# Local attention: probabilities times values on four 64x64 tiles, issued right behind the scores

## Chip, cores, metric

The kernel runs on 1 core of one Trainium2 chip. The time is device microseconds of one execution; lower is better. Engines are named as in the profile: PE is TensorE's matmul side, PEld its weight loads, DVE is VectorE, ACT ScalarE, POOL GpSimd, SP SyncE (it only issues DMAs here).

## The reference, cut to the part that is changed

The whole program is four layers on x of [8, 256, 128]: additive attention, a stack of six local-attention layers with feed-forward, a state-space layer and a mixture of experts. The change is in the stack. Per layer:

```python
qkv = x @ Wqkv                       # 16 heads of 64
q, k = l2norm(q) * qs, l2norm(k) * ksc
q = q * cos * scale + rotate_half(q) * sin * scale
k = k * cos * inv + rotate_half(k) * sin * inv
# windows of 32 positions; each sees itself and the window before it
sim = einsum('bhwie,bhwje->bhwij', bq, bk2) * 8.0
attn = softmax(where(mask, -max, sim), -1)
out = einsum('bhwij,bhwje->bhwie', attn, bv2)   # "mix" below
x = out.reshape(b, n, 1024) @ Wo + x            # then shift, layer norm, feed-forward with gelu
```

## The kernel before

Everything is float32, and the stream lies in SBUF transposed, channels on the 128 partitions. `local_attention` (L295) works in **units** of 512 tokens, which are two batches of 256. Four units a layer and six layers make 24 units, numbered i = 0 to 23. A unit is cut into eight **slots** j = 0 to 7, one per pair of heads. The program of every engine is written out by hand, slot by slot (`slot` at L529 for PE, L643 for ACT, L715 for POOL, L793 for DVE), each engine runs its list strictly in that order, and semaphores (`need`) tie the engines together. A hardware loop runs two units per turn; the first and the last unit stand outside it. A slot is a software pipeline in which four pairs of heads are in work at once:

- `scores(j)` (L439): two bf16 matmuls put the mask into PSUM banks 4 and 5 (L450), then 32 small float32 matmuls (L457), 64 rows by 32 columns of the array, add queries times keys. They wait for the rotated and normalised keys (`qk`) and for the probabilities of j-1, which leave the same banks.
- `project(j+2)` (L423): the two projection matmuls of 512 columns, q into bank 0 (L430) and k into bank 1 (L431). In slots 6 and 7 they belong to the next unit.
- `values(j+2)` (L406): the values of 128 tokens for half of the heads, four matmuls of 256 columns (L418), bank 2. Eight of them make the value tile `f_v` of a unit.
- `mix(j-2)` (L469): probabilities times values, 16 matmuls with 64 rows and 64 columns (L478), into bank 7.
- `turn(j-1)` (L462): four transposes of the probabilities (L466), bank 6.
- `norms(j+2)` (L433): the sums of squares of q and k, two matmuls of 512 columns (L436, L437), in banks 0 and 1 again. They need the squares that ACT makes of the copied projection.

Some slots carry work of the unit before (k = i-1) as well: slots 0 and 1 three matmuls each of the output projection (L491), slot 2 its last two and, on DVE, the residual and the token shift; slot 3 the mean of the layer norm (L498), slot 4 its variance (L504), slot 5 the first gate and hidden matmul (L511, L518), slot 6 two gates and a hidden, slot 7 a hidden and the second feed-forward matmul (L525). In slots 0 to 5 the order on PE is scores, project, values, mix, turn, norms. In slot 6 the mix stands ahead of the projection, in slot 7 the values do.

ACT does in a slot: `raw_copy` (L607, copies both projections out of PSUM, and L610 squares them), the exponential of the scores (L663) in place in banks 4 and 5, `value_copy` (L599), `out_copy` of the mix's result (L635), `spread` (L625, L626, L628: puts the transposed probabilities of the eight pairs of windows, 96 columns each, into `f_ptz`), and `inverse_norm` (L616 logarithm, L618 exponential). In slot 4 it then takes the logarithm and exponential of the variance (L678, L680).

DVE does in a slot: `soft_a` (L765 maximum, L769 subtraction), `normalise` (L757) of the next pair, `soft_b` (L776 sum, L779 reciprocal, L781 product, the probabilities), `rotate` (L747, L750); at the end of slot 2 L816 and the shift (L726, L728); at the end of slot 4 it scales the feed-forward input (L828), which waits for ACT's L680. POOL does the other half of the rotation (L709, L713).

## Time and profile before

| | |
|---|---|
| three runs | 2627.81, 2629.06, 2631.60 us; median 2629.06 |
| profiled execution, first to last instruction | 2628.3 us, inside the range of the runs; no other time is given for it |
| PE busy | 2396.4 us, 91% of the span |
| DVE / ACT / POOL busy | 1953.7 / 1795.4 / 1082.1 us |
| mean granted TensorE clock | 0.971 of full |

"Busy" is the union of an engine's instructions. A matmul's duration in a row is from its first read to a modelled end, so that consecutive rows overlap; the distance of two starts tells what the engine was held for. Each float32 matmul of the program is two PE instructions. In the timeline a row is a start and a duration in us, the engine, the line, the operation, the tiles, and in brackets the idle time just before it with what ended it. In the rows on windows each engine has its busy time and number of instructions, and PEclk is the granted clock as a share of 2.4 GHz.

### The profile page before, as it was taken

The page shows a single profiled execution, that of the slowest core. Times are in us where ns is not written, and L with a number is a line of the kernel's source. Part 1 is how long each engine was busy: PE and PEld are TensorE (multiplying, and loading weights), DVE is VectorE, ACT ScalarE, POOL GpSimd, SP SyncE. Part 2 cuts the span into 40 slices and gives each one's busy share as a digit, 9 for nine tenths or more (in the row PEclk, how much of TensorE's full clock was granted, in tenths as well). Part 3 has the DMA queues.
Part 4 walks back from the last instruction along what each step waited for, and adds up shares of the span by engine and source line. Part 5 has one row for each costly group of instructions (what it writes and reads, how often), then busy time and mean ns, then how long its engine had stood idle before and what let it go on. Part 6 is the DMA issues. An engine that isn't in the chain of part 4 may idle for free. (4 is left out here: it accounts for less than half of the span.)

```text
span 2628.3 us, 62460 instructions
## 1 busy us (share of the span) xinstructions
PE 2396.4 (91%) x24940; PEld 1259.7 (48%) x24940; DVE 1953.7 (74%) x2595; ACT 1795.4 (68%) x2593; POOL 1082.1 (41%) x461
## 2 busy tenths in 40 slices
PE   7799999999999999999999999999999877767778
PEld 2355555555554555555545455555555422222355
DVE  5678777788677777787778777788777658999542
ACT  4677767777677776777767777677677666545533
POOL 0354444444444444444444444444444204556130
PEclk8899999999999999999999999999999989999989
DMA  0100000000000000000000000000000010000001
GB/s 21 54 2 2 2 26 10 10 2 2 15 22 11 2 2 14 22 11 2 2 14 14 19 2 2 14 14 15 5 2 2 2 37 0 0 0 0 18 23 41
DMA packets 16047, 29.92 MB, mean 11 GB/s; under 512 B 3616, under 2 KB 6064, under 8 KB 15664
## 3 DMA queue, kind: packets, MB, share of 16 engines
q1 hardware_dynamic: 15760, 25.78, 3.1%
q8 instruction: 218, 3.57, 0.5%
q14 instruction: 69, 0.57, 0.1%
HBM read 24.73 MB, written 1.05 MB: 10 GB/s over the span
## 5 line engine op out<-in xcount | busy, mean ns | idle before, releaser
L709 POOL TENSOR_TENSOR f_rot<-f_raw,f_tabc 128x1024 f32<-128x1024 f32 x192 | 452.6, 2357 | 694.7 <-DVE f_qk L757 302.4
L713 POOL TENSOR_TENSOR f_rot<-f_rot,f_shuf 128x1024 f32<-128x1024 f32 x192 | 453.1, 2360 | 470.0 <-DVE f_shuf L750 470.0
L607 ACT ACTIVATE f_raw<-f_ps 128x1024 f32<-128x1024 f32 x192 | 196.5, 1023 | 324.9 <-PE f_ps L431 324.9
L478 PEld LDWEIGHTS f_ps<-f_ptz,f_v 64*64 64x64 f32 x6144 | 260.2, 133 | 93.7 <-issue 93.7
L478 PE MATMUL f_ps<-f_ptz,f_v 64*64 64x96 f32 (+1 forms) x6144 | 286.7, 243 | 1.5 <-ACT f_ptz L628 1.4
L776 DVE TENSOR_REDUCE f_sum<-f_ps 128x8 f32<-128x512 f32 x192 | 131.8, 686 | 185.6 <-ACT f_ps L663 185.5
L747 DVE STREAM_SHUFFLE f_shuf<-f_raw 128x1024 f32<-128x1024 f32 x192 | 255.2, 1329 | 0.0
L757 DVE SCALAR_TENSOR_TENSOR f_qk<-f_rn,f_rot 128x1024 f32<-128x1024 f32 x192 | 233.5, 1216 | 28.8 <-POOL f_rot L713 28.8
L430 PE MATMUL f_ps<-f_xs,f_wq 128*128 128x512 f32 x384 | 220.7, 657 | 24.3 <-DVE f_xs L728 21.0
L750 DVE TENSOR_TENSOR f_shuf<-f_shuf,f_tabs 128x1024 f32<-128x1024 f32 x192 | 236.7, 1233 | 7.6
L616 ACT ACTIVATE f_rn<-f_ps 128x1024 f32<-128x1024 f32 x192 | 198.8, 1035 | 39.5 <-PE f_ps L437 39.0
L618 ACT ACTIVATE f_rn<-f_rn,k_lift 128x1024 f32<-128x1024 f32 x192 | 220.6, 1149 | 6.3
L457 PE MATMUL f_ps<-f_qk 64*32 64x64 f32 x12288 | 195.1, 220 | 18.0 <-issue 18.0
L1136 POOL TENSOR_TENSOR s_prod<-s_state,s_cs 128x1024 f32<-128x1024 f32 x64 | 151.7, 2371 | 145.2 <-DVE s_state L1214 145.2
L418 PE MATMUL f_ps<-f_wv,f_xs 128*64 128x256 f32 x1536 | 210.5, 395 | 0.0
L765 DVE TENSOR_REDUCE f_max<-f_ps 128x8 f32<-128x512 f32 x192 | 131.8, 686 | 105.1 <-PE f_ps L457 103.7
L610 ACT ACTIVATE f_sq<-f_raw 128x1024 f32<-128x1024 f32 x192 | 203.1, 1058 | 6.1
L436 PE MATMUL f_ps<-f_sq,f_same 128*128 128x512 f32 x384 | 197.7, 597 | 6.2 <-ACT f_sq L610 6.2
L431 PE MATMUL f_ps<-f_xs,f_wk 128*128 128x512 f32 x384 | 203.1, 611 | 0.0
L437 PE MATMUL f_ps<-f_sq,f_same 128*128 128x512 f32 x384 | 197.0, 595 | 0.0
L457 PEld LDWEIGHTS f_ps<-f_qk 64*32 64x32 f32 x12288 | 161.9, 106 | 60.2 <-issue 60.2
L491 PE MATMUL f_ps<-f_o,f_wo 128*128 128x512 f32 x384 | 183.8, 612 | 0.0
(267 smaller groups left out, 3961.4 us busy)
## 6 DMA issues: line engine op xcount, KB each, us to landing
e_w<-in_e_w SPq DMA_DIRECT2D x16, 256.0 KB, 2.8
f_wq<-in_f_wq SPq DMA_DIRECT2D x12, 256.0 KB, 2.8
f_wk<-in_f_wk SPq DMA_DIRECT2D x12, 256.0 KB, 3.2
f_wv<-in_f_wv SPq DMA_DIRECT2D x12, 256.0 KB, 3.4
f_wo<-in_f_wo SPq DMA_DIRECT2D x6, 512.0 KB, 3.1
f_w<-in_f_w SPq DMA_DIRECT2D x6, 341.0 KB, 3.1
s_dx<-in_k_pick SPq DMA_DIRECT2D x1, 1536.0 KB, 9.3
f_w<-in_f_w SPq DMA_DIRECT2D x6, 192.0 KB, 3.8
```

The costliest lines, as they stand in the source:

```text
L418: mm = pe.matmul(view(ps, 2 * CH + 256 * r, [1, 256], p0=64 * h, rows=64), xs[:, at:at + 64], view(wv, CH * (q // 4) + 64 * h, [128, 4], [ ...
L430: pe.matmul(bank(0), wq[:, 128 * j:128 * j + 128], xs[:, :], start=True, stop=True)
L431: pe.matmul(bank(1), wk[:, 128 * j:128 * j + 128], xs[:, :], start=True, stop=True).then_inc(sem["a_mm"], 1)
L457: mm = pe.matmul(view(ps, (4 + h) * CH + (w // 4) * 64, [1, 64], p0=WIN * (w % 4), rows=WIN), t[64 * h:64 * h + 64, WIN * w:WIN * w + WIN] ...
L478: mm = pe.matmul(view(ps, 7 * CH + 64 * p, [1, n], p0=64 * h, rows=64), v[64 * h:64 * h + 64, p * CH + 64 * j:p * CH + 64 * j + 64], ptz[6 ...
L610: act.activation(sq[:, :], raw[:, :], ACT.Square).then_inc(sem["sq"], 1)
L618: act.activation(rn[:, :], rn[:, :], ACT.Exp, scale=-0.5, bias=con.lift).then_inc(sem["rn"], 1)
L709: pool.tensor_tensor(view(rot, 0, [S, 4], [1, S]), view(raw, 0, [S, 4], [1, S]), view(tab_c, 0, [S, 2], [0, 2], [1, S]), ALU.mult).then_in ...
L713: pool.tensor_tensor(rot[:, :], rot[:, :], shuf[:, :], ALU.add).then_inc(sem["rot"], 1)
L747: dve.stream_shuffle(shuf[:, :], raw[:, :], [(p + 16) % 32 for p in range(32)]).then_inc(sem["shuf"], 1)
L750: dve.tensor_tensor(view(shuf, 0, [S, 4], [1, S]), view(shuf, 0, [S, 4], [1, S]), view(tab_s, 0, [S, 2], [0, 2], [1, S]), ALU.mult).then_i ...
L757: dve.scalar_tensor_tensor(out=view(qk[j % 2], 0, [KOFF, 2], [1, UNIT]), in0=view(rn, 0, [UNIT, 2], [1, UNIT]), scalar=1e12, in1=view(rot, ...
```

## The change

The halves of the value tile hold batches now in place of alternating blocks of 64 tokens: partitions 0 to 63 hold batch 0, 64 to 127 batch 1. `values` computes 64 tokens of each batch for 512 channels, two matmuls of 512 columns in place of four of 256. In `mix` a matmul takes the rows of a batch half b and writes the columns of a head half h, four tiles (b, h) where there were two (h, h); the two batches go to different PSUM banks (6 and 7), each head sees four positions p in place of eight. Because bank 6 is also the target of `turn`, that now waits for the output copy. The scores, the mask and the softmax operands are arranged to match.

The order changes too. On PE `mix` stands right behind `scores` in every slot. On ACT `out_copy` and the exponential come first, ahead of `raw_copy`, and `value_copy` behind it in every slot.

```diff
             def values(i, q):
...
-                for r in range(2):
-                    for h in range(2):
-                        at = 128 * (q % 4) + 64 * r
-                        mm = pe.matmul(view(ps, 2 * CH + 256 * r, [1, 256], p0=64 * h, rows=64), xs[:, at:at + 64],
-                                       view(wv, CH * (q // 4) + 64 * h, [128, 4], [1, 64]),
-                                       start=(r == 0), stop=True, skip_group_check=True)
+                for b in range(2):
+                    at = S * b + 64 * (q % 4)
+                    mm = pe.matmul(view(ps, 2 * CH, [1, CH], p0=64 * b, rows=64), xs[:, at:at + 64],
+                                   wv[:, CH * (q // 4):CH * (q // 4) + CH], start=True, stop=True)
             def turn(i, j):
...
+                need(pe, sem["o"], i * 8 + j)
             def mix(i, j):
...
-                for p in range(8):
-                    n = 96 if p < 7 else 64
+                for p in range(4):
+                    n = 96 if p < 3 else 64
                     for h in range(2):
-                        mm = pe.matmul(view(ps, 7 * CH + 64 * p, [1, n], p0=64 * h, rows=64),
-                                       v[64 * h:64 * h + 64, p * CH + 64 * j:p * CH + 64 * j + 64],
-                                       ptz[64 * h:64 * h + 64, 96 * p:96 * p + n],
-                                       start=(p == 0), stop=(p == 7), skip_group_check=True)
+                        for b in range(2):
+                            mm = pe.matmul(view(ps, (6 + b) * CH + S * b + 64 * p, [1, n], p0=64 * h, rows=64),
+                                           v[64 * b:64 * b + 64, p * INNER + 128 * j + 64 * h:p * INNER + 128 * j + 64 * h + 64],
+                                           ptz[64 * b:64 * b + 64, 96 * (4 * h + p):96 * (4 * h + p) + n],
+                                           start=(p == 0), stop=(p == 3), skip_group_check=True)
             def slot(i, j, run, more, before):
...
                 if run:
                     scores(i, j)
+                if had2:
+                    mix(u2, b2)
...
-                if j == 6 and had2:
-                    mix(u2, b2)
...
-                if j != 6 and had2:
-                    mix(u2, b2)
...
             def value_copy(i, q):
...
-                act.activation(view(v, 2 * (q % 4) * CH + 256 * (q // 4), [CH, 2], [1, 256]),
-                               view(ps, 2 * CH, [256, 2], [1, 256]), ACT.Copy).then_inc(sem["v"], 1)
+                act.activation(view(v, INNER * (q % 4) + CH * (q // 4), [1, CH]), bank(2), ACT.Copy).then_inc(sem["v"], 1)
             def out_copy(i, j):
...
-                act.activation(o[:, UNIT * j:UNIT * j + UNIT], bank(7), ACT.Copy).then_inc(sem["o"], 1)
+                act.activation(view(o, UNIT * j, [S, 2], [1, S]), view(ps, 6 * CH, [CH + S, 2], [1, S]),
+                               ACT.Copy).then_inc(sem["o"], 1)
             def slot(i, j, run, more, before):
...
+                if had2:
+                    out_copy(u2, b2)
+                if run:
+                    need(act, sem["shift"], i * 8 + j + 1)
+                    act.activation(view(ps, 4 * CH, [CH, 2], [1, S]), view(s[j % 2], 0, [S, 2], [1, S]),
+                                   ACT.Exp, scale=8.0).then_inc(sem["exp"], 1)
                 if has:
                     raw_copy(u, a)
...
-                if has and j == 5:
-                    value_copy(u, a)
-                if run:
-                    need(act, sem["shift"], i * 8 + j + 1)
-                    act.activation(view(ps, 4 * CH, [CH, 2], [64, 4], [1, 64]), view(s[j % 2], 0, [64, 2], [128, 4], [1, 64]),
-                                   ACT.Exp, scale=8.0).then_inc(sem["exp"], 1)
-                if has and j != 5:
+                if has:
                     value_copy(u, a)
...
-                if had2:
-                    out_copy(u2, b2)
                 if had1:
                     spread(u1, b1)
```

Left out of the diff: the scores' place in banks 4 and 5 (`(2 * four + b) * 64` in place of `(w // 4) * 64`), the matching views in the two subtractions and products on DVE, and the order of the four mask blocks.

PE, slot 5 of a unit, before. L450 and L457 are the scores, L430 and L431 the projection, L418 the values, L478 the mix, L466 the turn, L436 and L437 the norms.

```order
L450 MATMUL f_ps<-f_maskb,f_identb 128x256 x2
L457 MATMUL f_ps<-f_qk 32x64 x32
L430 MATMUL f_ps<-f_xs,f_wq 128x512
L431 MATMUL f_ps<-f_xs,f_wk 128x512
L418 MATMUL f_ps<-f_wv,f_xs 64x256 x4
L478 MATMUL f_ps<-f_ptz,f_v 64x96 x14
L478 MATMUL f_ps<-f_ptz,f_v 64x64 x2
L466 MATMUL f_ps<-f_ident,f_s 128x128 x4
L292 REGISTER_ALU
L436 MATMUL f_ps<-f_sq,f_same 128x512
L437 MATMUL f_ps<-f_sq,f_same 128x512
```

The same slot in the changed kernel, where line numbers are a few lower: L448 and L456 are the scores, L479 the mix, L428 and L429 the projection, L417 the values, L434 and L435 the norms.

```order
L448 MATMUL f_ps<-f_maskb,f_identb 128x256 x2
L456 MATMUL f_ps<-f_qk 32x64 x32
L479 MATMUL f_ps<-f_ptz,f_v 64x96 x12
L479 MATMUL f_ps<-f_ptz,f_v 64x64 x4
L428 MATMUL f_ps<-f_xs,f_wq 128x512
L429 MATMUL f_ps<-f_xs,f_wk 128x512
L417 MATMUL f_ps<-f_wv,f_xs 64x512 x2
L466 MATMUL f_ps<-f_ident,f_s 128x128 x4
L292 REGISTER_ALU
L434 MATMUL f_ps<-f_sq,f_same 128x512
L435 MATMUL f_ps<-f_sq,f_same 128x512
```

The mix has moved from between values and turn to the place between scores and projection; between the projection and the norms only values and turn are left.

ACT, end of slot 4 (L678, L680) and slot 5, before. L607 and L610 are the raw copy and its square, L599 the value copy, L663 the exponential of the scores, L669 the layer norm's scale, L635 the output copy, L625 the first of the spread.

```order
L678 ACTIVATE f_sq<-f_ps,k_eps 128x512
L680 ACTIVATE f_sq<-f_sq 128x512
L292 REGISTER_ALU
L607 ACTIVATE f_raw<-f_ps 128x1024
L610 ACTIVATE f_sq<-f_raw 128x1024
L599 ACTIVATE f_v<-f_ps 128x2x256
L663 ACTIVATE f_ps<-f_s 128x2x256
L669 ACTIVATE f_xn<-f_xn,f_fcol 128x512
L635 ACTIVATE f_o<-f_ps 128x512
L625 ACTIVATE f_ptz<-f_ps 128x8x32
```

The same place in the changed kernel: L675 and L677 are the variance's steps, L633 the output copy, L657 the exponential, L605 and L608 the raw copy and square, L598 the value copy, L623 the spread.

```order
L675 ACTIVATE f_sq<-f_ps,k_eps 128x512
L677 ACTIVATE f_sq<-f_sq 128x512
L633 ACTIVATE f_o<-f_ps 128x512
L657 ACTIVATE f_ps<-f_s 128x2x256
L292 REGISTER_ALU
L605 ACTIVATE f_raw<-f_ps 128x1024
L608 ACTIVATE f_sq<-f_raw 128x1024
L598 ACTIVATE f_v<-f_ps 128x512
L668 ACTIVATE f_xn<-f_xn,f_fcol 128x512
L623 ACTIVATE f_ptz<-f_ps 128x8x32
```

The output copy and the exponential have moved ahead of the raw copy. DVE's and POOL's lists are the same as before.

## Rows read from the trace of the kernel before

**Rows 1.** The page: busy time, share of span and instructions of each engine

```profile
PE 2396.4 (91%) x24940; PEld 1259.7 (48%) x24940; DVE 1953.7 (74%) x2595; ACT 1795.4 (68%) x2593; POOL 1082.1 (41%) x461
```

**Rows 2.** Windows: one unit, from its first scores to the next unit's; columns as named

```profile
core 0: us, PE busy (x) PEld busy (x) DVE busy (x) ACT busy (x) POOL busy (x), PEclk, DMA share, GB/s
...
248.96:330.91 81.95, 79.75 (x983) 43.57 (x982) 64.97 (x92) 62.22 (x91) 37.76 (x16) 1.00 0.01 2
```

**Rows 3.** Groups of instructions: busy us, mean ns of one, idle before

```profile
L478 PE MATMUL f_ps<-f_ptz,f_v 64*64 64x96 f32 (+1 forms) x6144 | 286.7, 243 | 1.5 <-ACT f_ptz L628 1.4
...
L418 PE MATMUL f_ps<-f_wv,f_xs 128*64 128x256 f32 x1536 | 210.5, 395 | 0.0
...
L457 PE MATMUL f_ps<-f_qk 64*32 64x64 f32 x12288 | 195.1, 220 | 18.0 <-issue 18.0
...
L635 ACT ACTIVATE f_o<-f_ps 128x512 f32<-128x512 f32 x192 | 112.4, 585 | 4.9 <-PE f_ps L478 4.8
...
L599 ACT ACTIVATE f_v<-f_ps 128x512 f32<-128x512 f32 x192 | 111.0, 578 | 0.0
```

**Rows 4.** Timeline of one unit, from the end of slot 4 through slot 5

```profile
297.45 1.05 ACT L616 ACTIVATE f_rn<-f_ps 128x1024 f32<-128x1024 f32 x1
...
297.88 0.38 PE L450 MATMUL f_ps<-f_maskb,f_identb 128*128 128x256 bf16 x2
...
300.08 1.02 PE L431 MATMUL f_ps<-f_xs,f_wk 128*128 128x512 f32 x2
...
300.29 0.63 ACT L680 ACTIVATE f_sq<-f_sq 128x512 f32<-128x512 f32 x1
...
300.95 1.92 DVE L828 TENSOR_TENSOR f_xn<-f_cen,f_sq 128x512 f32<-128x512 f32 x1 [1.13 <-ACT f_sq L680]
...
301.14 1.02 ACT L607 ACTIVATE f_raw<-f_ps 128x1024 f32<-128x1024 f32 x1 [0.22 <-PE f_ps L431]
...
302.05 1.49 PE L478 MATMUL f_ps<-f_ptz,f_v 64*64 64x96 f32 x32
...
302.80 0.68 DVE L765 TENSOR_REDUCE f_max<-f_ps 128x8 f32<-128x512 f32 x1
...
303.46 0.66 PE L466 MATMUL f_ps<-f_ident,f_s 128*128 128x128 f32 x4
...
303.96 1.02 PE L436 MATMUL f_ps<-f_sq,f_same 128*128 128x512 f32 x2
...
304.23 0.60 ACT L663 ACTIVATE f_ps<-f_s 128x512 f32<-128x512 f32 x1 [0.50 <-DVE f_s L769]
```

**Rows 5.** Timeline of a slot of the first unit, which has no mix

```profile
109.23 1.02 PE L431 MATMUL f_ps<-f_xs,f_wk 128*128 128x512 f32 x2
...
110.29 1.02 ACT L607 ACTIVATE f_raw<-f_ps 128x1024 f32<-128x1024 f32 x1 [1.29 <-PE f_ps L431]
...
112.45 1.12 PE L436 MATMUL f_ps<-f_sq,f_same 128*128 128x512 f32 x2 [0.60 <-ACT f_sq L610]
```

**Rows 6.** Timeline: slot 3 and next scores, slot 6 projection, slot 7

```profile
281.70 1.02 PE L431 MATMUL f_ps<-f_xs,f_wk 128*128 128x512 f32 x2
...
286.48 1.02 PE L436 MATMUL f_ps<-f_sq,f_same 128*128 128x512 f32 x2
...
289.24 0.38 PE L450 MATMUL f_ps<-f_maskb,f_identb 128*128 128x256 bf16 x2 [0.87 <-DVE f_s L781]
...
312.66 1.12 PE L430 MATMUL f_ps<-f_xs,f_wq 128*128 128x512 f32 x2 [0.56 <-DVE f_xs L728]
...
322.51 1.02 PE L431 MATMUL f_ps<-f_xs,f_wk 128*128 128x512 f32 x2
...
326.24 1.02 PE L436 MATMUL f_ps<-f_sq,f_same 128*128 128x512 f32 x2
```

**Rows 7.** Timeline and windows at the loop's back edge; PEclk is the granted clock

```profile
334.14 0.41 PE L457 MATMUL f_ps<-f_qk 64*32 64x64 f32 x11 [2.07 <-issue]
...
335.20:338.40 3.20, 3.20 (x8) 1.00 (x8) 1.90 (x3) 0.47 (x1) 0.00 (x0) 0.50 0.02 5
```

More of the change, by code:

```diff
@@ L456, in scores @@
                                 else view(t, KOFF + WIN * (w - 1), [1, 2 * WIN], p0=64 * h, rows=64))
-                        mm = pe.matmul(view(ps, (4 + h) * CH + (w // 4) * 64, [1, 64], p0=WIN * (w % 4), rows=WIN),
+                        four, b = w // 4 % 2, w // 8
+                        mm = pe.matmul(view(ps, (4 + h) * CH + (2 * four + b) * 64, [1, 64], p0=WIN * (w % 4), rows=WIN),
                                        t[64 * h:64 * h + 64, WIN * w:WIN * w + WIN], keys, start=False, stop=True,
@@ L768, in soft_a @@
                 need(dve, sem["t_mm"], i * 8 + j - 1)
-                dve.tensor_tensor(view(t, 0, [64, 2], [128, 4], [1, 64]), view(ps, 4 * CH, [CH, 2], [64, 4], [1, 64]),
+                dve.tensor_tensor(view(t, 0, [S, 2], [64, 4], [1, 64]), view(ps, 4 * CH, [CH, 2], [64, 4], [1, 64]),
                                   view(mx, 0, [4, 2], [1, 4], [0, 64]), ALU.subtract).then_inc(sem["shift"], 1)
@@ L780, in soft_b @@
                 need(dve, sem["rcp"], i * 8 + j + 1)
-                dve.tensor_tensor(view(t, 0, [64, 2], [128, 4], [1, 64]), view(ps, 4 * CH, [CH, 2], [64, 4], [1, 64]),
+                dve.tensor_tensor(view(t, 0, [S, 2], [64, 4], [1, 64]), view(ps, 4 * CH, [CH, 2], [64, 4], [1, 64]),
                                   view(rc, 0, [4, 2], [1, 4], [0, 64]), ALU.mult).then_inc(sem["p"], 1)
@@ L1582, in constants @@
     first = seen & (own | (np.arange(128)[:, None] >= WIN))
-    k["k_mask"] = np.concatenate([np.where(z, f(0), f(NEG)) for z in (first, seen, first, seen)], 1)
+    k["k_mask"] = np.concatenate([np.where(z, f(0), f(NEG)) for z in (first, first, seen, seen)], 1)
     k["k_ones2"] = np.full((C, C), 1.0 / DN, f)
```

## The prediction

> **What bounds the kernel now.** I began with the page's busy times. TensorE (PE) is busy 91% of the span, VectorE (DVE) 74%, ScalarE (ACT) 68% [rows 1]. That is an average over all stages, so the next view was one whole unit of the local attention, by windows: of 81.95 us PE works 79.75, DVE 64.97, ACT 62.22 [rows 2]. 24 such units make up most of the span. PE sets the pace, but only 2.2 us a unit is free there, so the question is less how much matmul time goes away than whether PE still has work while it waits for the others.
>
> The groups of instructions give the prices. The mix (L478) is 32 PE instructions a call, 6144 in all, and the values (L418) 8 a call, 1536 in all [rows 3]. Then I read the timeline of slot 5 of one unit. Three things are to be seen there [rows 4]. PE goes from the second projection matmul (L431, 300.08) to the norms (L436, 303.96) in 3.88 us and never waits, because values, mix and turn lie between. ACT copies the projection (L607) at 301.14, 1.06 after L431. And DVE is late: it can only scale the feed-forward input (L828, 300.95) after ACT's second exponential for it (L680), so the maximum of the scores (L765) starts at 302.80 and ACT's Exp (L663) at 304.23, three microseconds behind the raw copy. Today nobody minds.
>
> **The mix.** Its 32 instructions now use two diagonal tiles at a time, hence 16 rounds, in 302.05 to 303.46 = 1.41 us [rows 4]. On four tiles it is 8 rounds. One matmul's row is 243 ns long [rows 3] though a round comes every 1.41/16 = 88 ns, so about 0.15 us of filling and draining does not halve: 0.15 + 1.26/2 = 0.78, and I take 0.77, a saving of 0.64 a call. Bounds: 0.60 (the drain hidden too) and 1.41 (the halves of the rows do not run together). The nearest row is the scores, 64 instructions on eight tiles in 195.1/192 = 1.02 us, 16 ns each [rows 3]; 32 at that rate would be 0.51, so neither issue nor weight loads hold 0.77 back.
>
> The Trainium skill (TensorEngine Tiling (Array Packing), Performance Considerations, on the PSUM bottleneck) says that tiling speeds up TensorE but not the emptying of PSUM, which may become the bound. No number here depends on it; it speaks against the change, and the rows say where: in the chain from projection through ACT to norms below.
>
> **The values.** Four matmuls of 256 columns on two tiles become two of 512: per tile the same columns. I cost it at nothing, between -0.1 (four fewer weight loads) and +0.05. Copies keep their element counts: ACT's value copy is 578 ns with its two pieces and the one-piece output copy 585 ns [rows 3], so swapping the forms costs nothing either.
>
> **What the move does.** The mix now stands between scores and projection, so between L431 and the norms only values and turn are left. The first unit, which has slots without a mix, shows that price: L431 at 109.23, raw copy 110.29, norms at 112.45 after a wait of 0.60 [rows 5]. So the norms cannot come sooner than 3.22 after L431, of which 2.16 run from the start of the raw copy. On ACT the output copy and the Exp now come ahead of the raw copy. Slot by slot, against today:
>
> - Slots 0 and 1: three output-projection matmuls each cover the chain. Only the mix shortens: 2 x -0.64 = -1.28.
> - Slots 2 and 4: today 3.88 from L431 to norms [rows 4]; then 0.77 ahead and 3.22 behind, 3.99. +0.11 each, +0.22.
> - Slot 3: today 286.48 - 281.70 = 4.78 (the mean matmul is in it), and 0.87 more is lost at the next scores, which wait for the probabilities [rows 6]. The early Exp frees DVE sooner, so that wait goes; DVE's long residual work before this slot still makes the Exp late, and I allow 0.9 of hold on the raw copy: 0.77 + 3.22 + 0.9 - 4.78 - 0.87 = -0.76.
> - Slot 5: the Exp starts 304.23 - 297.45 = 6.78 after the previous logarithm (L616), on a chain that the change leaves alone (L616, L618, two steps on ACT, L828, maximum and subtraction on DVE). The raw copy follows 0.54 later, the norms 2.16 after that: 9.48, against 303.96 - 297.45 = 6.51 today [rows 4, 5]. +2.97; the logarithm comes some 0.15 sooner since the spread no longer delays it. +2.8.
> - Slot 6: the mix was ahead of the projection already, which waits 0.56 for DVE there [rows 6]. The shorter mix mostly widens the wait: -0.1.
> - Slot 7: today 326.24 - 322.51 = 3.73 from L431 to norms [rows 6], then 0.77 + 3.22: +0.26, with the Exp a little in the way +0.3.
>
> Sum: -1.28 + 0.22 - 0.76 + 2.8 - 0.1 + 0.3 = +1.2 us a unit. 23 units have a feed-forward behind them: +27. The first unit and the tail are within a microsecond of nothing.
>
> The new wait of the turn for the output copy (both share a PSUM bank now) costs nothing: that copy comes first on ACT, and PE has projection and values in between. Queued behind it would be norms; if the cover went it would cost the copy's 0.58 a slot. No DMA is added, and none stands behind a moved step: SP's weight loads wait on the same counts, and on POOL nothing moves.
>
> **The clock.** In slot 5 L431 would start 300.08 - 297.45 + 0.77 = 3.4 after the logarithm; values and turn take PE to 2.4 behind that (112.45 - 0.60 - 109.23 = 2.6 with the drain [rows 5]), and the norms start at 9.3: PE would idle some 3.4 us. At a loop's back edge PE stalls 2.07 us today, and soon after the granted clock is 0.50 (1.2 GHz) for 3.2 us in which PE is busy throughout [rows 7]. Such a stretch costs 3.2/2 = 1.6 us. Now one stall longer than that comes in every unit. Part of the slow stretch falls into the stall itself and part into the wait of slot 6, so between 0 and 1.6; I take 1.2: 23 x 1.2 = +28. The Trainium skill (TensorE: Matmul & The Clock Gate, Part 1, on HAM oscillation) has the same rule, that waits inside a loop make the clock fall again and again, and the trace agrees. By it the sum is what stands here; if it did not hold, the second rival's.
>
> **Sum.** 2628.3 (the span, which lies within the three run times and 0.8 under their median) + 27 + 28 = 2683.
>
> **The rivals.**
> 1. Order costs, clock stays: stalls fall so that the clock is kept, or the slow stretch is absorbed. For: slot 6 has slack. Against: 3.4 us is well over the 2.07 that was enough. 2629 + 27 = 2656.
> 2. Faster. Place: ACT's Exp of slot 5. If it did not hold the raw copy (DVE reaching the maximum over 3 us sooner because all its work before has moved up), slot 5 would be like slot 4, +0.11 in place of +2.8, and the unit -1.5: 23 x -1.5 = -35, and 2594. It decides at a hold of about 1.7 us instead of 2.97. For: the early Exp does help DVE elsewhere (slot 3). Against: the scaling on DVE waits for ACT's L680 of the same unit, and that chain starts from slot 4's own norms [rows 4]. The Trainium skill (TensorEngine Tiling, Theoretical Speedup) promises up to 2x for each small dimension; taken as the kernel's gain it would be the full 0.64 of each of 192 calls, 123 us, and 2506, only if nothing waited anywhere.
> 3. The change does not do what it says: the four tiles don't overlap and the mix stays at 1.41. Slots 0, 1, 2, 4 and 7 lose 0.64 each, 3.2 a unit, 23 x 3.2 = 74 more: 2757. Against: the scores already run on both row halves at 16 ns each [rows 3].
>
> **How the numbers follow.** Forecast with both terms 0.66, rival 1 0.15, rival 2 0.10, rival 3 0.05; nearly no change 0.04 (a mix of 0.60, no clock loss and a smaller hold). A measurement here tells about 0.2%, 5 us, from no change. Slower: 0.66 + 0.15 + 0.05 = 0.86; same 0.04; faster 0.10. Forecast alone: 2660 to 2715 (mix 0.65 to 0.95, clock term 10 to 38). The range takes in rival 1 and the upper bounds, 2645 to 2728, and leaves out rivals 2 and 3.
>
> **What would show it.** Right: the mix's start to the projection near 0.8 us; a wait of PE at the norms for ACT's square of about 0.8 in slots 2 and 4 and over 3 us in slot 5, 23 times, some 70 us in the list of waits where today almost nothing stands; in slot 5 Exp directly followed by the raw copy; granted clock 0.50 once a unit; slots 0 and 1 shorter by 0.6. Wrong: the maximum of slot 5 starting over a microsecond sooner after the scores than today's 4.9, a mix near 1.4, or the clock staying at 1.00 through slot 5.

## Result, and the profile after

| | before | changed |
|---|---|---|
| median of 16 runs each (range) | 2629.22 us (2625.89 to 2633.24) | 2637.7 us (2632.13 to 2643.09) |
| ratio, 95% interval | | 1.0031 (1.0023 to 1.0038) |
| profiled span | 2628.3 | 2639.8 |
| PE busy | 2396.4 | 2311.3 |
| mean granted clock | 0.971 | 0.968 |

The change makes the kernel slower by 0.3%, 8.5 us. The sign was forecast and the size was not: 2683 with a range of 2645 to 2728 stood against 2637.7. The profiled execution of the changed kernel (2641.6 us) lay 4 us above its median.

The page's busy times, to be held against [rows 1]:

```profile
PE 2311.3 (88%) x24172; PEld 1099.1 (42%) x24172; DVE 1965.7 (74%) x2595; ACT 1815.4 (69%) x2593; POOL 1085.4 (41%) x461
```

PE works 85 us less, in 768 instructions fewer, and the kernel is still slower: all of that gain and more has become waiting. Two of the page's groups (against [rows 3]) and the list of waits tell where:

```profile
L434 PE MATMUL f_ps<-f_sq,f_same 128*128 128x512 f32 x384 | 216.1, 645 | 137.2 <-ACT f_sq L608 137.2
...
L417 PE MATMUL f_ps<-f_wv,f_xs 128*64 128x512 f32 x768 | 207.3, 618 | 0.0
```

```profile
PE f_ps L434 <- ACT f_sq L608: 137.2, 124, 2.2
```

PE now waits 124 times, 137 us in all, at the norms for ACT's square of the raw copy. Windows of the same unit as [rows 2], and of a stretch in slot 5 of the next unit:

```profile
248.32:330.92 82.60, 75.66 (x951) 36.77 (x950) 65.31 (x91) 62.69 (x91) 37.86 (x16) 1.00 0.01 2
...
387.60:390.80 3.20, 3.20 (x5) 1.14 (x5) 3.15 (x4) 1.86 (x5) 1.86 (x2) 0.50 0.07 23
```

The unit has grown from 81.95 to 82.60 us while PE's work in it fell by 4.1. In the other unit the granted clock is 0.50 while PE is busy throughout.

The length of a slot is the distance between the starts of two successive scores. Medians over the units, in us:

| slot | 0 | 1 | 2 | 3 | 4 | 5 | 6 | 7 | sum |
|---|---|---|---|---|---|---|---|---|---|
| before | 10.42 | 10.52 | 9.51 | 9.84 | 8.65 | 9.58 | 11.89 | 11.24 | 81.65 |
| changed | 9.79 | 9.79 | 9.91 | 9.84 | 8.90 | 11.10 | 11.66 | 11.62 | 82.6 |
| forecast | -0.64 | -0.64 | +0.11 | -0.76 | +0.11 | +2.8 | -0.1 | +0.3 | +1.2 |
| measured | -0.63 | -0.73 | +0.40 | 0.00 | +0.25 | +1.52 | -0.23 | +0.38 | +0.95 |

Slot 5 stands there with its clock kept. In 15 of the units it runs at the low clock and takes 12.79, 1.69 more. The two profiles then differ by three terms and a small one:

| | us |
|---|---|
| order and tiles, 22 units of +0.95 | +21 |
| low clock in slot 5, 15 x 1.69 | +25 |
| what the slots around the loop's ten back edges (where the loop jumps back) take above their medians: 37.8 behind them and 6.9 just before them, now 9.7 and 1.0 | -34 |
| first unit (68.36 to 66.36) | -2 |

That is +10 of the 11.5 between the spans; the last unit adds the rest. The third row is larger than either of the others and stands nowhere in the prediction.

Over half of that row is clock. Of the 37.8 us behind the edges before, 18 are idle time of PE and 19 are lost to a low granted clock, in nine of the ten edges; of the 9.7 in the changed kernel 6 are idle and nothing is lost to the clock. So the low clock has mostly moved, from the back edges to slot 5 (19 us before, 25 after), which is why its mean falls only from 0.971 to 0.968.

Slots 4 and 5 in the timeline of the changed kernel, against [rows 4]:

```profile
295.89 1.02 ACT L614 ACTIVATE f_rn<-f_ps 128x1024 f32<-128x1024 f32 x1
296.40 2.36 POOL L710 TENSOR_TENSOR f_rot<-f_rot,f_shuf 128x1024 f32<-128x1024 f32 x1 [1.23 <-DVE f_shuf L747]
...
296.55 0.38 PE L448 MATMUL f_ps<-f_maskb,f_identb 128*128 128x256 bf16 x2
...
297.81 0.84 PE L479 MATMUL f_ps<-f_ptz,f_v 64*64 64x96 f32 x32
...
298.58 1.12 PE L428 MATMUL f_ps<-f_xs,f_wq 128*128 128x512 f32 x2
298.70 0.63 ACT L677 ACTIVATE f_sq<-f_sq 128x512 f32<-128x512 f32 x1
...
299.37 0.69 DVE L825 TENSOR_TENSOR f_xn<-f_cen,f_sq 128x512 f32<-128x512 f32 x1 [3.11 <-ACT f_sq L677]
...
299.54 1.02 PE L429 MATMUL f_ps<-f_xs,f_wk 128*128 128x512 f32 x2
...
299.98 0.68 DVE L762 TENSOR_REDUCE f_max<-f_ps 128x8 f32<-128x512 f32 x1
...
301.42 0.60 ACT L657 ACTIVATE f_ps<-f_s 128x512 f32<-128x512 f32 x1 [1.60 <-DVE f_s L766]
...
301.96 1.01 ACT L605 ACTIVATE f_raw<-f_ps 128x1024 f32<-128x1024 f32 x1
...
304.10 1.12 PE L434 MATMUL f_ps<-f_sq,f_same 128*128 128x512 f32 x2 [1.95 <-ACT f_sq L608]
```

The mix holds PE from 297.81 to 298.58, the 0.77 worked out ahead. Exp and raw copy follow each other 0.54 apart and the norms come 2.14 behind, also as worked out. What is new is DVE's scaling L825: 0.69 us, where L828 took 1.92 in [rows 4].

### The profile page after: what moved, and what is told of

Same layout as the page of the kernel before. It is cut to its first block and busy times, and to the rows that moved or that the text cites. A ratio compares the mean times of both kernels' runs of the same rounds, so it can differ in the third digit from the quotient of the medians.

```text
span 2639.8 us, 60924 instructions
## 1 busy us (share of the span) xinstructions
PE 2311.3 (88%) x24172; PEld 1099.1 (42%) x24172; DVE 1965.7 (74%) x2595; ACT 1815.4 (69%) x2593; POOL 1085.4 (41%) x461
## 5 line engine op out<-in xcount | busy, mean ns | idle before, releaser
L706 POOL TENSOR_TENSOR f_rot<-f_raw,f_tabc 128x1024 f32<-128x1024 f32 x192 | 454.0, 2364 | 871.4 <-ACT f_raw L605 796.7
L434 PE MATMUL f_ps<-f_sq,f_same 128*128 128x512 f32 x384 | 216.1, 645 | 137.2 <-ACT f_sq L608 137.2
L747 DVE TENSOR_TENSOR f_shuf<-f_shuf,f_tabs 128x1024 f32<-128x1024 f32 x192 | 274.3, 1429 | 7.6
L605 ACT ACTIVATE f_raw<-f_ps 128x1024 f32<-128x1024 f32 x192 | 195.6, 1019 | 78.2 <-PE f_ps L429 78.2
L428 PE MATMUL f_ps<-f_xs,f_wq 128*128 128x512 f32 x384 | 214.4, 640 | 25.8 <-ACT f_gate L639 18.8
L435 PE MATMUL f_ps<-f_sq,f_same 128*128 128x512 f32 x384 | 208.4, 626 | 0.0
L608 ACT ACTIVATE f_sq<-f_raw 128x1024 f32<-128x1024 f32 x192 | 203.2, 1058 | 6.1
L417 PE MATMUL f_ps<-f_wv,f_xs 128*64 128x512 f32 x768 | 207.3, 618 | 0.0
L657 ACT ACTIVATE f_ps<-f_s 128x512 f32<-128x512 f32 x192 | 115.3, 601 | 131.0 <-DVE f_s L766 129.3
L429 PE MATMUL f_ps<-f_xs,f_wk 128*128 128x512 f32 x384 | 197.0, 595 | 0.0
L456 PE MATMUL f_ps<-f_qk 64*32 64x64 f32 x12288 | 191.6, 220 | 0.0
L456 PEld LDWEIGHTS f_ps<-f_qk 64*32 64x32 f32 x12288 | 160.5, 106 | 40.8 <-issue 40.8
L479 PE MATMUL f_ps<-f_ptz,f_v 64*64 64x96 f32 (+1 forms) x6144 | 164.5, 243 | 12.7 <-issue 5.2
L633 ACT ACTIVATE f_o<-f_ps 128x512 f32<-128x512 f32 x192 | 112.8, 588 | 86.4 <-PE f_ps L479 43.4
```

What stands on the lines that cost most here:

```text
L417: mm = pe.matmul(view(ps, 2 * CH, [1, CH], p0=64 * b, rows=64), xs[:, at:at + 64], wv[:, CH * (q // 4):CH * (q // 4) + CH], start=True, st ...
L428: pe.matmul(bank(0), wq[:, 128 * j:128 * j + 128], xs[:, :], start=True, stop=True)
L434: pe.matmul(bank(0), same_head[:, :], sq[:, 0:UNIT], start=True, stop=True)
L435: pe.matmul(bank(1), same_head[:, :], sq[:, UNIT:], start=True, stop=True).then_inc(sem["n_mm"], 1)
L456: mm = pe.matmul(view(ps, (4 + h) * CH + (2 * four + b) * 64, [1, 64], p0=WIN * (w % 4), rows=WIN), t[64 * h:64 * h + 64, WIN * w:WIN * w ...
L608: act.activation(sq[:, :], raw[:, :], ACT.Square).then_inc(sem["sq"], 1)
```

## The experiments

### Order and tiles apart

**order_only**: the kernel before, its two-tile mix and its values in four matmuls kept, with the new order on PE and ACT alone. On PE:

```diff
                 if run:
                     scores(i, j)
+                if had2:
+                    mix(u2, b2)
...
-                if j != 6 and had2:
-                    mix(u2, b2)
```

and on ACT the output copy and the exponential ahead of `raw_copy`, as in the change.

> The kernel before (two diagonal tiles for the mix, values in four matmuls) with the changed kernel's order on PE and ACT. Theory 1 (the loss comes from the order: fewer matmuls between projection and norms, and the Exp ahead of the raw copy): slots 2, 3, 4, 5 and 7 as in the changed kernel plus the 0.65 us by which the mix is longer, slots 0 and 1 as before (10.4): about 82.6 + 7 x 0.65 = 87 us a unit, and some 2750 us in all, well slower than both kernels. The stall at the loop's back edge stays long (3 to 5 us in slot 0) if it goes by the number of PE instructions ahead of the loop, and is short (about 1 us) if it is the mix's new place behind the scores that covers it. Rival (the order costs nothing and the four tiles themselves are what disturbs): within 0.5% of the kernel before.

Measured: 2745.19 us, ratio 1.043 (1.0414 to 1.0446). Slots 10.44, 10.55, 10.55, 9.84, 9.71, 11.09, 12.48, 12.28. PE waits 124 times at the norms, as in the changed kernel, for 107.1 us; the back edges cost 33.8, nearly as before.

The order costs 4.3% by itself; the four tiles, with the values in two matmuls, pay back nearly all of it. Slots 0, 1, 2, 4, 6 and 7 gain 0.6 to 0.8 each from the tiles; slots 3 and 5 gain none (9.84 both, 11.09 and 11.10): there the norms wait for DVE and ACT, and a shorter mix only widens the wait (from 0.84 to 1.51 and from 1.29 to 1.94). About 23 us come from the back edges (33.8 to 9.7, and nothing to 1.0 before them), and the low clock in slot 5, which order_only never has, takes 25 back. The rival that the tiles themselves disturb is out. No run has the four tiles in the old order, so what they are worth there isn't shown.

**vals4**: the changed kernel with its values again in four matmuls of 256 columns.

```diff
+                    for c in range(2):
-                    mm = pe.matmul(view(ps, 2 * CH, [1, CH], p0=64 * b, rows=64), ...
+                        mm = pe.matmul(view(ps, 2 * CH + 256 * c, [1, 256], p0=64 * b, rows=64), ...
```

> The changed kernel with the values in four matmuls of 256 columns again, in the new layout. Theory 1 (values cost the same either way; only the number of PE instructions moves the stall at the loop's back edge): slots outside the edges unchanged within 0.05 us, the extra in slot 0 after a back edge goes from 0.5 to 1.5 us to something else, 3 to 5 us if the old alignment comes back (+20 to +35 us). Rival (the two wide matmuls are cheaper by themselves, or the edge gain is from the order): every slot longer by 0.1, or no difference at all at the edges (within 5 us).

Measured: 2654.22 us, ratio 1.0091 (1.0077 to 1.0104). The slots are those of the changed kernel (slot 5: 11.09) but for 0.05 in slot 4 and 0.11 in slot 7, 5 us over the units. But the back edges cost 32.3 in place of 9.7. In the profiles these 23 us are the only large term that makes vals4 slower; against them, 4 units in place of 15 have slot 5 at the low clock, which varies from one execution to the next (below). So nearly all that the fewer instructions bring, they bring where the loop turns.

### The exponential ahead of the raw copy

**exp5** puts the raw copy ahead of the Exp again in slot 5, **exp35** in slots 3 and 5.

```diff
+                if has and j in (3, 5):
+                    raw_copy(u, a)
                 if run:
                     need(act, sem["shift"], i * 8 + j + 1)
...
-                if has:
+                if has and j not in (3, 5):
                     raw_copy(u, a)
```

> The changed kernel with ACT's raw copy ahead of the Exp in slot 5 only. Theory 1 (the Exp holds the raw copy, PE then waits 1.95 us at the norms, and that stall is what lowers the clock): the wait in slot 5 falls to about 0.6, the slot to 9.7 us, and the slow stretches of 1.7 us in 15 of 23 units go: 23 x 1.35 + 15 x 1.7 = 57 us less than the changed kernel, about 2581 us. Rival (the chain through the norms' logarithm or DVE holds slot 5 anyway, or the clock falls all the same): less than 20 us.

> As exp5, and the raw copy ahead of the Exp in slot 3 too. Theory 1: the 1.50 us that PE waits at slot 3's norms falls to 0.6 at most, but the Exp then comes late for the probabilities that the next scores wait for, as in the kernel before (0.87 there): between 0 and 0.9 us a unit less than exp5, 0 to 20 us. Rival: the probabilities are held so much longer that it is no faster than exp5.

Measured: exp5 2591.33 us, ratio 0.9846 (0.9831 to 0.9861), slot 5 9.76, and no unit with slot 5 at the low clock in place of 15. That is 46 us less than the changed kernel where 57 were expected: slot 5 (29) and the clock (25) came nearly as expected, while the first unit took 4 us more, for a reason that no run shows, and the back edges 3. exp35 2580.19 us, ratio 0.9814 (0.9799 to 0.9829): 1.9% faster than the kernel before, and the best of the study. Its page and three rows of its timeline:

```profile
PE 2287.0 (89%) x24172; PEld 1088.7 (42%) x24172; DVE 1964.5 (76%) x2595; ACT 1817.3 (71%) x2593; POOL 1083.0 (42%) x461
```

```profile
285.85 0.38 PE L448 MATMUL f_ps<-f_maskb,f_identb 128*128 128x256 bf16 x2 [0.25 <-DVE f_s L780]
...
292.92 1.12 PE L434 MATMUL f_ps<-f_sq,f_same 128*128 128x512 f32 x2 [1.46 <-ACT f_sq L608]
...
301.81 1.12 PE L434 MATMUL f_ps<-f_sq,f_same 128*128 128x512 f32 x2 [0.61 <-ACT f_sq L608]
```

In slot 5 (301.81) the wait is 0.61, the same as in the slots without a late Exp. Slot 3 falls from 9.84 in the changed kernel to 8.49, but 0.9 of it comes back in slot 4 (292.92, a wait of 1.46, slot 4 from 8.90 to 9.77). So the forecast's mechanism in slot 5 is shown: the Exp, late behind DVE, held the raw copy and with it the norms, and once it doesn't, the clock is kept too. exp5 makes the condition of the prediction's second rival true, which put that case at 2594, but that the time agrees is luck: the rival took 1.5 us off a unit, exp5 takes off 0.37 (81.65 to 81.28, 8 us over the units), and some 31 us come from the back edges.

### The step in slot 5 that was mis-sized

**scale_more**: the changed kernel with two more products of the same shape, whose results nobody reads, ahead of DVE's scaling.

```diff
+                    for h in range(2):
+                        dve.tensor_tensor(junk[:, h * UNIT:h * UNIT + UNIT], cen[:, :], sq2[:, :], ALU.mult)
                     dve.tensor_tensor(xn[:, :], cen[:, :], sq2[:, :], ALU.mult).then_inc(sem["scaled"], 1)
```

> The changed kernel with two more products of the same size (into a scratch tile that nobody reads) ahead of DVE's scaling in slot 4: 1.3 us of work there, about what the scaling lost in the kernel before. Theory (the prediction's chain was right and only this duration off): the Exp and with it the raw copy and norms of slot 5 come 1.2 to 1.3 us later, slot 5 is 12.3 us without a slow stretch, PE's stall there 3.2 us, and a slow stretch comes in nearly every unit: 23 x 1.25 = 29 us and some 8 to 20 stretches of 1.7 us more, 2670 to 2700 us, about what was predicted for the change. Rival (the stall of slot 5 is set by something else and takes the extra work in): under 10 us.

Measured: 2680.22 us, ratio 1.0198 (1.0178 to 1.0218). Its timeline in slot 5:

```profile
300.90 1.29 DVE L827 TENSOR_TENSOR f_junk<-f_cen,f_sq 128x512 f32<-128x512 f32 x2 [3.12 <-ACT f_sq L678]
...
302.11 0.69 DVE L828 TENSOR_TENSOR f_xn<-f_cen,f_sq 128x512 f32<-128x512 f32 x1
...
304.15 0.60 ACT L658 ACTIVATE f_ps<-f_s 128x512 f32<-128x512 f32 x1 [2.81 <-DVE f_s L767]
304.69 1.01 ACT L606 ACTIVATE f_raw<-f_ps 128x1024 f32<-128x1024 f32 x1
...
306.84 2.08 PE L435 MATMUL f_ps<-f_sq,f_same 128*128 128x512 f32 x2 [3.15 <-ACT f_sq L609]
```

DVE is 1.2 us later, the wait at the norms is 3.15 where it was 1.95, and the norms run at the low clock (2.08 us where a full-clock row has 1.12). With the 1.2 us that the forecast had counted on DVE put back, the time is 2680, against 2683 forecast. That is no proof of the whole sum, and the match is partly luck: against the kernel before, order and tiles come to +48 here (22 units of 83.82 against 81.65), the low clock to +30 and the back edges to -33 (10.1 and 1.6 are left). It does show that the chain in slot 5 passes DVE's time on to PE: slot 5 goes from 11.09 to 12.29. A longer stall also drops the clock oftener: 18 units in this profile, and a mean granted clock of 0.961 to 0.962 in its four runs, against 0.967 to 0.972 in the sixteen of the changed kernel.

**scale_psum** asks why L828 took 1.92 before and 0.69 after. The kernel before, with ACT's second exponential for the scale written to PSUM bank 3 in place of SBUF.

```diff
-                    act.activation(sq2[:, :], sq2[:, :], ACT.Exp, scale=-0.5).then_inc(sem["rs2"], 1)
+                    act.activation(bank(3), sq2[:, :], ACT.Exp, scale=-0.5).then_inc(sem["rs2"], 1)
...
-                    dve.tensor_tensor(xn[:, :], cen[:, :], sq2[:, :], ALU.mult)
+                    dve.tensor_tensor(xn[:, :], cen[:, :], bank(3), ALU.mult)
```

> The kernel before with the reciprocal root of slot 4 written to PSUM bank 3 in place of SBUF, so that DVE's scaling (L828) reads one operand from PSUM. Theory (its 1.93 us was 0.69 of work and 1.24 of contention with POOL's L713 for SBUF, which ran at the same time and no longer does in the changed kernel): about 0.69 in all 24, with POOL still running. Rival (it waits for something else, or is slow by its operands): stays at 1.9. The time of the kernel hardly moves (within 0.2%), since nobody waits for DVE there before.

Measured: 2609.94 us, ratio 0.9918 (0.9899 to 0.9938). The instruction in the view of its tile (shortest, median, longest in ns), in the kernel before, in the changed one and in scale_psum:

```profile
L828 DVE TENSOR_TENSOR f_xn<-f_cen,f_sq x24: 692/1928/1943, 219.3 to 2103.4; 128x512 f32<-128x512 f32 x24
```

```profile
L825 DVE TENSOR_TENSOR f_xn<-f_cen,f_sq x24: 691/693/693, 216.8 to 2115.5; 128x512 f32<-128x512 f32 x24
```

```profile
L828 DVE TENSOR_TENSOR f_xn<-f_cen,f_ps x24: 686/687/691, 220.5 to 2082.7; 128x512 f32<-128x512 f32 x24
```

And what POOL did at that time, before and in scale_psum:

```profile
299.97 2.35 POOL L713 TENSOR_TENSOR f_rot<-f_rot,f_shuf 128x1024 f32<-128x1024 f32 x1 [2.07 <-DVE f_shuf L750]
```

```profile
300.48 2.36 POOL L713 TENSOR_TENSOR f_rot<-f_rot,f_shuf 128x1024 f32<-128x1024 f32 x1 [2.06 <-DVE f_shuf L750]
...
301.42 0.69 DVE L828 TENSOR_TENSOR f_xn<-f_cen,f_ps 128x512 f32<-128x512 f32 x1 [1.09 <-ACT f_ps L680]
```

Before, L828 (300.95 to 302.87 [rows 4]) runs beside POOL's product (299.97 to 302.32), both with both operands in SBUF, and takes 1.92. With one operand in PSUM it runs beside the same POOL product and takes 0.69. In the changed kernel POOL is done at 298.76, before L825 starts at 299.37, and it takes 0.69 from SBUF. So the 1.92 was the price of company, not of the operation. It ends 0.55 behind POOL's product, little less than its own 0.69: it spent nearly the whole time waiting for POOL to end. The time was expected unchanged, which was a miss, and fell by 0.8%: slot 5 barely gains (9.58 to 9.51), but slot 6 goes from 11.89 to 11.21. That slot's projection waited 0.61 (median) for DVE's shift [rows 6], and the wait is gone; somebody did wait for DVE.

### Other orders

**late23457** (the changed kernel): in slots 2, 3, 4, 5 and 7 the mix behind the projection and the turn behind the norms on PE; on ACT raw copy, Exp, value copy, output copy, logarithm, spread. **late2_exp35**: exp35 with this order in slot 2 alone.

```diff
+                late = j in (2, 3, 4, 5, 7) and run and has
-                if had2:
+                if had2 and not late:
                     mix(u2, b2)
...
                     project(u, a)
+                    if had2 and late:
+                        mix(u2, b2)
...
-                if had1:
+                if had1 and not late:
                     turn(u1, b1)
                 if has:
                     norms(u, a)
+                if had1 and late:
+                    turn(u1, b1)
```

> A version to beat both: in slots 2, 3, 4, 5 and 7 PE does scores, projection, mix, values, norms and then the turn; ACT does raw copy and square, Exp, value copy, output copy, logarithm, spread. By theory 1 the 3.22 us from projection to norms now cover mix and values: against exp35 (2580 us) a slot loses the 0.77 us of the mix ahead and gains the 0.43 of the turn behind, 5 x 0.34 = 1.7 us a unit, 39 us: about 2541. If the later Exp makes the next scores wait for the probabilities, as in exp35's slot 3 to 4, 0 to 20 us of it are given back: 2541 to 2565. Rival (another engine, ACT first, is the bound by now): no faster than 2575.

> exp35 with, in slot 2 alone, the mix behind the projection and the turn behind the norms: in late23457 slot 2 took 9.41 in place of 9.91 us and the loss lay in slots 3, 5 and 0. If the two add up, 0.5 us a unit less than exp35: about 2569 us. If slot 2's later probabilities move slot 3 instead, no gain on 2580.

Measured: 2590.78 us, ratio 0.985 (0.9831 to 0.9868), far from the 2541 expected; slot 2 is shorter by 0.5 (9.41), but slots 3 to 5 come out at 9.96, 8.84 and 9.99, and the back edges cost more (14.9, and 9.4 in the slots before them). late2_exp35 took 2604.04 us, ratio 0.9899 (0.9881 to 0.9916): slot 2 gains its 0.5, slot 3 grows from 8.49 to 9.96. In late23457 the slots add up to 80.71, against 80.79 in exp35: what some save, others lose, and the 11 us by which it is slower lie at the back edges (24 against 12, with the slots before them). In late2_exp35 slot 3 loses three times what slot 2 gains: the mix there waits 0.75 for ACT's spread, which comes later behind the later turn, and the next scores wait 0.93 in place of 0.25 for DVE's probabilities. Neither beats exp35, and both expectations of a gain missed.

### The back edge

Here the loop jumps from the end of an even unit to the start of an odd one. [Rows 7] showed 2.07 us of stall in the second set of matmuls behind it. The changed kernel has no such stall at the same edge; its mix takes 1.22 us in place of 0.84, its weight loads breaking off once for 0.23, and the slot is 0.65 longer than usual:

```profile
332.37 1.22 PE L479 MATMUL f_ps<-f_ptz,f_v 64*64 64x96 f32 x32
...
333.25 0.20 PEld L479 LDWEIGHTS f_ps<-f_ptz,f_v 64*64 64x64 f32 x5 [0.23 <-issue]
```

The page lists the transfers of instructions (q8), here of the changed kernel and of pad_in32:

```profile
q8 instruction: 207, 3.39, 0.5%
```

```profile
q8 instruction: 229, 3.75, 0.6%
```

Before it is 218. The loop makes eleven turns, so 11 transfers more are one more per turn; all of the difference lies in the stack (203 transfers there before, 192 in the changed kernel, 214 in pad_in32), and each is of 16 KB. Two readings stood against each other: the amount of code in a turn, or its place in memory. Waits on a semaphore that has long been reached add instructions to PE's list and cost next to no time (two waits share one instruction; pad_in's slots are those of the changed kernel). pad_after (89 waits) and pad_after178 (178) have them once, ahead of the loop, in the changed kernel; pad_before (181) in the kernel before:

```diff
-            pe.wait_ge(sem["const"], n_const)
+            for _ in range(89):
+                pe.wait_ge(sem["const"], n_const)
```

pad_in (8), pad_in16 (16) and pad_in32 (32) have them at the end of each slot of the changed kernel:

```diff
                 if before and j == 7:
                     w2_mm(k)
+                for _ in range(8 if run else 0):
+                    pe.wait_ge(sem["const"], n_const)
```

> The changed kernel with 89 extra waits on an already reached semaphore in PE's program ahead of the loop; the loop itself is the same to the instruction. Theory A (the stall at the loop's back edge goes by where the loop lies in PE's program, in fetched blocks): the extra of slot 0 after the ten back edges, 9.7 us in all in the changed kernel, comes back to some 30 us, as where the values are four matmuls, and the kernel is 15 to 30 us slower. Theory B (it goes by the number of instructions inside the loop): edges stay at about 10 us, time within 5 us of the changed kernel.

> The kernel before with 181 such waits ahead of the loop. Theory A: the extra at the edges, 37.8 us in slot 0 of ten units, moves clearly, to 10 to 20 us if a block holds 256 instructions, and the kernel is up to 25 us faster for an edit that does nothing. Theory B: edges stay between 33 and 42 us and the time within 5 us of before.

> The changed kernel with 8 extra waits on an already reached semaphore at the end of each slot of PE's program: the loop of two units is 128 PE instructions longer, as many as the four-matmul values add there, and no matmul is added. Theory B (the stall after a back edge goes by what the loop itself holds): the extra of slot 0 over the ten edges goes from about 10 us to 25 to 40 us, and the kernel is 10 to 30 us slower. If the extra stays near 10 to 15 us, the bare number of instructions is not it either, and what the four-matmul values bring back at the edge stays open.

> The changed kernel with 16 extra waits at the end of each slot; two waits share an instruction (pad_in's 8 came out as 4), so 8 instructions a slot and 128 a turn of the loop. Theory C (what counts is how many blocks of instructions one turn of the loop has to fetch: the kernels with four-matmul values show 218 instruction transfers, those with two 207, eleven fewer for eleven turns): the transfers go to about 218 and the extra of slot 0 over the ten edges to 25 to 40 us. If the transfers stay at 207 or 208, the edges stay near 10 to 15 us.

> As pad_in16 with 32 waits, 16 instructions a slot and 256 a turn, 16 KB, the mean size of one transfer. Theory C: about 11 more transfers than the changed kernel (218) and the extra at the edges above 25 us. Rival (the edge goes by the matmuls themselves): edges stay at 10 to 15 us although the transfers are more.

> The changed kernel with 178 waits, 89 instructions, ahead of the loop (pad_after had 44): PE's loop starts just where it starts in the kernel before, and only the loop's own length differs. Theory A (the loop's place): the extra over the edges 30 us or more. Theory C: 207 transfers, 10 to 18 us.

Measured, with the sum over ten back edges of what the first slot takes above its median, the number of PE's instructions (matmuls, weight loads and the added waits) that the trace shows ahead of the loop and in one turn of it, and the page's transfers:

| kernel | ahead | in a turn | transfers | back edges, us | time, us | ratio |
|---|---|---|---|---|---|---|
| changed | 2052 | 3967 | 207 | 9.7 | 2637.7 | 1.0031 |
| pad_after | 2096 | 3967 | 207 | 14.9 | 2636.8 | 1.0025 (1.0015 to 1.0035) |
| pad_after178 | 2140 | 3967 | 208 | 26.5 | 2653.71 | 1.0106 (1.0067 to 1.0146) |
| pad_in | 2084 | 4031 | 208 | 14.6 | 2640.7 | 1.0044 (1.0028 to 1.0059) |
| pad_in16 | 2116 | 4095 | 218 | 33.3 | 2654.22 | 1.0099 (1.0072 to 1.0126) |
| vals4 | 2132 | 4095 | 218 | 32.3 | 2654.22 | 1.0091 |
| before | 2132 | 4095 | 218 | 37.8 | 2629.22 | |
| pad_before | 2222 | 4095 | 219 | 44.4 | 2639.86 | 1.0034 (1.0023 to 1.0045) |
| pad_in32 | 2180 | 4223 | 229 | 46.9, and 19.3 in the slots before | 2681.08 | 1.02 (1.0181 to 1.0219) |

The other runs fit: order_only and scale_psum, with the instructions of the kernel before, have 33.8 and 32.8; exp5, exp35, late2_exp35 and scale_more, with those of the changed kernel, 10.1 to 11.5, and late23457 14.9.

vals4 settles where the term comes from: the 768 matmuls fewer, with their weight loads, are worth 23 us at the edges. By which of their two effects is not settled, because they do two things at once. They take 128 instructions out of a turn, and they move the start of the loop by 80. The start alone bears much of it: with the turn left as it is, 9.7 becomes 14.9 and 26.5 as the start moves by 44 and 88, and the time of pad_after178 is that of vals4, at 208 transfers. A longer turn at about the same start (pad_after178 to vals4) adds only 6. But every run with a longer turn has a later start too, and no run lengthens the turn alone. So the count of transfers goes with the stall (33 at 218 in pad_in16 and vals4, two unlike kernels, 46.9 at 229), but is not its rule, and the rule stays open. The trace doesn't show what PE waits for either: at the edge of [rows 7] a transfer runs from 331.23 to 332.67 and is done before the stall ends at 334.14, and the changed kernel has one there too.

Of the expectations, theory B was right for pad_after. pad_before moved the edges up where theory A wanted them down and B unchanged. pad_in was a miss: eight waits a slot are only 64 instructions a turn. pad_in16 came out as theory C said. pad_in32 got 22 transfers more where 11 were expected. pad_after178 fell between A and C; its profile is of the shortest of four runs that range from 2643 to 2666 us, so its 26.5 is rather too small than too large.

Beside this, the number of low-clock stretches differs from one execution to the next: the sixteen runs of the changed kernel have a mean granted clock of 0.967 to 0.972. pad_after's profile (0.972) has four in slot 5 where the changed kernel's (0.968) has 15, with the same slots (11.09). A stretch is 1.69 us, so this alone is some 19 us between two such executions; a single profile of this kernel tells its clock term badly.

## Why the prediction was wrong, and where it was right

- **The mix**: right. 0.84 busy for 32 instructions, 0.77 from its start to the projection; 164.5 us in all where it was 286.7. The rival that the tiles do not overlap is out. The chain from projection through ACT to norms became the limit, with 124 waits there. The Trainium skill (TensorEngine Tiling (Array Packing), Performance Considerations) warns that tiling does not speed up the emptying of PSUM. The trace doesn't bear out that this was the bound here: order_only has the same 124 waits with the two-tile mix, so the order made them, and the tiles only widened those of slots 3 and 5.
- **The values**: right, nearly nothing in the slot: from their start (L417, 291.59) to the turn (292.60) 1.01 us, where L418 held PE for 1.02. The vals4 run shows what was overlooked: the instructions that they save count at the back edge.
- **Slots 0, 1, 6, 7**: right to 0.13. **Slots 2 and 4**: +0.40 and +0.25 for +0.11; the wait at the norms is 0.61 as in [rows 5], and L429 to the norms takes 3.23 where 3.22 was worked out, so the step was sound and small. 0.10 of the rest is that behind such a wait the second matmul of the norms follows 0.96 behind the first, in place of 0.86.
- **Slot 3**: -0.76 forecast, 0.00 measured. The wait at the next scores went, as forecast. The allowance of 0.9 for the late Exp was too small: from L429 (280.80) to the norms it is 5.03, a hold of 1.81 on top of the 3.22. The raw copy starts 0.54 behind an Exp that had waited 2.45 for DVE, and the norms wait 1.50 in place of 0.60.

```profile
283.14 0.60 ACT L657 ACTIVATE f_ps<-f_s 128x512 f32<-128x512 f32 x1 [2.45 <-DVE f_s L766]
283.68 1.01 ACT L605 ACTIVATE f_raw<-f_ps 128x1024 f32<-128x1024 f32 x1
...
285.83 1.12 PE L434 MATMUL f_ps<-f_sq,f_same 128*128 128x512 f32 x2 [1.50 <-ACT f_sq L608]
```

- **Slot 5**: +2.8 forecast, +1.52 measured. The step has the Exp start 6.78 after the previous logarithm, "on a chain that the change leaves alone". The chain was the right one, but its L828 was not left alone. From the logarithm to the norms it is 304.10 - 295.89 = 8.21, against 9.48 worked out; 1.23 of the 1.27 between them is L828, 1.92 before and 0.69 now, since it no longer meets POOL's product. scale_psum shows the cause and scale_more that the rest of the chain stands. The prediction's own sign of being wrong came true here: the maximum starts 3.43 behind the scores (299.98 - 296.55), 1.49 sooner than today's 4.92.
- **Order, summed**: +27 forecast, +21 measured. Slots 3 and 5 erred in opposite ways, so this came out better than its parts, by luck. The list of waits has 137 us where some 70 were forecast: 45 in slot 5, 35 in slot 3, 22 in slot 7 and 15 each in slots 2 and 4.
- **The clock**: +28 forecast (23 x 1.2), +25 in this profile, but by other factors: 15 x 1.69. PE's stall is 1.95 in slot 5, not 3.4, and the clock falls in some units and not in others; how many is a matter of the execution, so that +25 comes near +28 partly by luck. The forecast also left out that the low clock at the back edges, which it had read in [rows 7], could go. The rule of the Trainium skill (TensorE: Matmul & The Clock Gate, Part 1, on HAM oscillation), that waits inside a loop make the clock fall again and again, agrees with the trace in 15 of the units; in exp5, where the wait is 0.61, no unit has its slot 5 at the low clock. The first rival, with the clock kept (2656), had the clock too good and also knew nothing of the back edge; it, and not the second, is what the sum without the clock term gives.
- **What failed**: the working reads [rows 7] for the price of a stall and costs a change of that stall, and of the low clock behind it, at nothing, neither in the sum nor among the rivals. It is no constant of the kernel: 37.8 + 6.9 us before, 9.7 + 1.0 after, -34 in all, with -2 in the first unit. Without this term the sum of what was measured is 2628.3 + 21 + 25 = 2674, inside the range; with it 2638. The two terms forecast came to 55 and measured 46; the missing one is nearly four times that error. That the sign still came out is luck: nothing in the working kept the missing term (36 us) smaller than the other two (46).

## What to carry to other kernels

A shorter matmul pays only in the stages where its engine doesn't already wait; where cover goes away with it, look at the order of the engine that feeds it: here an Exp ahead of a raw copy, in two of eight slots, cost 57 us of 2638. A duration carried over from the old trace holds only as long as what runs beside it does: look at what the neighbour engines do in that moment, before and after. And this loop, with long unrolled code, has a stall at its back edge that goes with how many instructions stand in it and ahead of it; when an edit removes or adds hundreds of them, compare the first slot behind the edge with its median, before and after. The page's count of instruction transfers is a hint and no more: pad_after178 cost 16 us at one transfer more.

## What the runs showed of the hardware

- Two products of float32 tiles from SBUF, one on DVE and one on POOL, got in each other's way: DVE's took 1.93 us in place of 0.69. With one of DVE's operands in PSUM it took 0.69 beside the same work on POOL. Using that alone made the kernel before 0.8% faster. DVE's instruction waited for the end of POOL's: L828 ended 0.55 behind it, and in four slots of the second unit of the changed kernel L747 (128x1024) ended 1.07 to 1.09 behind POOL's L706, whether it took 1.31, 1.57, 1.85 or 1.94. DVE's L747 in slot 2 of the changed kernel (276.44, beside POOL's L706 from 274.92 to 277.28) takes 1.93, where L750, the same operation, takes 1.22 without POOL (298.60 in the kernel before).
- The first slot behind the loop's back edge takes 1.7 to 5.1 us above its median in the kernel before, each of ten times, and 1 us on average in the changed one. Before, half of it is idle time of PE and half low granted clock.
- On four 64x64 tiles the 32 float32 instructions of the mix hold PE for 0.77 us, on two for 1.41.
- A stall of PE of 1.94 us was enough for the granted clock to fall to 0.50, but not every time: after 1.95 in slot 5 of one unit (304.10) it stayed at 1.00, after 1.94 in the next it had fallen, as the row shows, 1.94 us long where it is 1.12 at full clock:

```profile
387.35 1.94 PE L434 MATMUL f_ps<-f_sq,f_same 128*128 128x512 f32 x2 [1.94 <-ACT f_sq L608]
```
